# Two transformer layers in one kernel: the first attention stage, with its floor rows, small roots, key low parts and transfers put in another order

## The reference, cut to what matters

```python
x = x + L0_xattn(layernorm(x), ctx, ctx, ...)   # first stage: gated (mLSTM) attention
x = x + L0_ffn(layernorm(x), ...)               # silu(x wg) * (x wu), then wd
x = x + L1_xattn(layernorm(x), ctx, mask, ...)  # relu projections, softmax, weighted values
x = x + L1_ffn(layernorm(x), ...)               # ternary weights, two hidden layers

# inside L0_xattn, for each of 16 sequences and 8 heads:
ig, fg = (concat(q, k, v) @ w.T + b)                      # the gates
cs = cumsum(log_sigmoid(fg)); log_D = cs[s] - cs[t] + ig[t], causal
D = exp(log_D - max);  C = (q k^T / sqrt(32)) * D
h = C / (maximum(|sum C|, exp(-max)) + 1e-6) @ v          # exp(-max) is the "floor"
out = layernorm(h) * ln_scale
```

## Time and profile before

| | us |
|---|---|
| median of 3 runs (lowest, highest) | 562.78 (562.52, 564.67) |
| the profiled execution | 560.74 |
| its span, first to last instruction | 559.0 |
| TensorE busy | 538.2 |
| VectorE, ScalarE, GpSimd busy | 319.1, 243.4, 72.5 |

### The profile page before, as it was taken

One profiled execution on the slowest core, in us unless ns is written; L12 is line 12 of the kernel. 1 busy time (PEld: TensorE's weight loads), 2 busy tenths in 40 slices (PEclk: granted clock), 3 DMA queues, 4 the chain that ended last, 5 costly groups with the idle time before them and its releaser, 6 DMA issues.

```text
span 559.0 us, 8453 instructions
## 1 busy us (share of the span) xinstructions
PE 538.2 (96%) x2773; PEld 451.8 (81%) x2773; DVE 319.1 (57%) x776; ACT 243.4 (44%) x456; POOL 72.5 (13%) x116
## 2 busy tenths in 40 slices
PE   7899898999999999999999999999999999999996
PEld 5677777888998888778888788889788889788886
DVE  6678788868777689652443543434542543633333
ACT  6446657758798633551122441122541122631111
POOL 5232443204210441000000000000000000000000
PEclk9999999999999999999999999999999999999999
DMA  6693636356958776000000000000000000000001
GB/s 174 195 262 113 163 85 173 94 215 203 403 166 278 259 241 204 0 1 1 0 2 9 28 2 1 0 1 21 18 0 1 0 1 33 6 1 0 1 0 40
DMA packets 29860, 47.44 MB, mean 85 GB/s; under 512 B 3392, under 2 KB 21184, under 8 KB 29440
## 3 DMA queue, kind: packets, MB, share of 16 engines
q1 hardware_dynamic: 24848, 30.14, 17.1%
q0 software_dynamic: 4848, 16.78, 9.4%
q10 hardware_dynamic: 128, 0.05, 0.0%
HBM read 40.27 MB, written 2.10 MB: 76 GB/s over the span
## 4 chain that ended last, share of the span: by engine, by line
PE 59%; issue 8%; POOL 2%; DVE 1%; POOLq 0%; DVEq 0%
PE ps L953 58%; POOL rstd L457 1%; POOL h L575 1%; PE ps L609 0%; PE ps L917 0%; DVE qr L1595 0%; DVE x L1583 0%; DVE xn L1345 0%; DVE alT L1622 0%; DVE xT L1352 0%; POOL w L564 0%; POOLq L575 0%; POOL w L566 0%; PE ps L908 0%; DVE ot L1675 0%
## 5 line engine op out<-in xcount | busy, mean ns | idle before, releaser
L1308 ACT ACTIVATE h<-ps,scol 128x512 f32<-128x512 f32 x64 | 44.2, 690 | 175.3 <-PE ps L953 175.2
L953 PE MATMUL ps<-hBt,h 128*128 128x512 f32 x512 | 117.5, 390 | 0.0
L953 PE MATMUL ps<-hA,h 128*128 128x512 f32 x512 | 117.3, 390 | 0.0
L953 PEld LDWEIGHTS ps<-hA,h 128*128 128x128 f32 x512 | 95.9, 188 | 20.4 <-DVE hA L1649 0.6
L953 PEld LDWEIGHTS ps<-hBt,h 128*128 128x128 f32 x512 | 95.8, 188 | 20.3 <-DVE hBt L1649 0.6
L953 PE MATMUL ps<-xT,w 128*128 128x512 f32 x256 | 61.7, 396 | 1.0 <-DVE xT L1352 1.0
L953 PEld LDWEIGHTS ps<-xT,w 128*128 128x128 f32 x256 | 46.1, 188 | 14.9 <-issue 6.0
L1667 DVE CAST hBt<-h 128x512 fp32r<-128x512 f32 x32 | 13.7, 427 | 73.7 <-ACT h L1308 73.7
L1667 DVE CAST hA<-h 128x512 fp32r<-128x512 f32 x32 | 13.7, 427 | 70.0 <-ACT h L1308 70.0
L457 POOL TENSOR_TENSOR rstd<-ve,mhalf 128x4 f32<-128x4 f32 x16 | 16.4, 1028 | 263.1 <-DVE ve L1340 263.1
L1291 ACT ACTIVATE silD<-ps,scol 128x512 f32<-128x512 f32 x32 | 22.1, 689 | 45.1 <-PE ps L953 45.1
(11 more groups left out here) (180 smaller groups left out, 881.7 us busy)
## 6 DMA issues: line engine op xcount, KB each, us to landing
looked<-w_all_in SPq DMA_DIRECT2D x16, 704.0 KB, 5.9
h<-w_all_in POOLq DMA_DIRECT2D x16, 512.0 KB, 6.9
V<-ctx_in SPq DMA_DIRECT2D x8, 512.0 KB, 4.8
Qb<-xT SPq DMA_DIRECT2D x64, 64.0 KB, 2.0
w<-w_all_in POOLq DMA_DIRECT2D x3, 1024.0 KB, 7.0
x<-x_in SPq DMA_DIRECT2D x4, 512.0 KB, 4.7
kstA<-ctxT_in SPq DMA_DIRECT2D x4, 512.0 KB, 4.8
kstC<-ctxT_in SPq DMA_DIRECT2D x4, 512.0 KB, 6.9
```

Source lines behind the costliest of these rows:

```text
L953: last = mm(o, a, b, start=(k == 0 and p == 0), stop=(k == n_k - 1 and p == 1))
L1308: fn(h32[:, m % 2, :], ps[:, 2 + m % 4, :], ACT.Gelu, scale=scol[:, L + 1, m:m + 1])\
```

## The change

Six things move, and nothing is computed otherwise.

1. TensorE: `turn_e` of the next group stands behind the last scores of `q` = 3 instead of ahead of its exponent tiles. VectorE: `floor_copy` stands right ahead of the first `weigh` of `q` = 3 instead of behind `finish` in `q` = 2.
2. GpSimd: the layer norm's `nmean`, root and `shift`, and `h_root(Q*g, 0)`, stand ahead of the wait for the gates and of `pieces` instead of behind.
3. `k_lo` is two instructions of 512 columns, each with its semaphore, and the gates' keys wait for each half by itself.
4. SyncE: `x` of the last two groups is loaded ahead of the second keys instead of behind the first queries.
5. SyncE, in the loop: the queries of `q` = 2 stand ahead of the keys' load instead of behind.
6. SyncE, in the loop: the values' load stands behind the queries of `q` = 3 instead of ahead.

```diff
             sp.dma_start(diag[:, :], diag_in).then_inc(s["consts"], 16)
+            for g in range(2, G):
+                sp.dma_start(x[:, Q * g:Q * g + Q, :], x_in[Q * g:Q * g + Q].rearrange("b s d -> s b d"))\
+                    .then_inc(s["x_rest"], 16)
             sp.wait_ge(s["klo_done"], 1)
...
+                    queries_in(g, u, 2)
                     with sp.If(i < 1):
 
                         sp.wait_ge(s["klo_done"], 2 + u)
...
-                    queries_in(g, u, 2)
-                    def early():
+                    if u == 0:
                         gates_in(gn)
+                    else:
+                        with sp.If(i < 1):
+                            gates_in(gn)
+                    queries_in(g, u, 3)
+                    def following():
                         sp.wait_ge(s["pv_done"], Q * g + 2)
                         values(gn, 1 - u)
+                        lead_in(gn, 1 - u)
...
+            def k_lo_apart(n, u):
+
+                pool.wait_ge(s["khi_done"], n + 1)
+                for c, name in ((0, "klo_first"), (1, "klo_done")):
+                    nc.gpsimd.tensor_tensor(kT[:, u, 1, c, :], kstA[:, c, :], kT[:, u, 0, c, :], ALU.subtract)\
+                        .then_inc(s[name], 1)
...
                     if c == KD:
+                        pe.wait_ge(s["klo_first"], g + 1)
+                    if c == KD + 1:
                         pe.wait_ge(s["klo_done"], g + 1)
```

## The result

| | before | changed |
|---|---|---|
| median, 21 runs each (us) | 562.75 | 565.39 |
| lowest, highest | 559.08, 565.73 | 562.63, 568.07 |
| span of the profiled execution | 559.0 | 564.9 |
| granted TensorE clock, mean | 0.999 | 0.991 |

The ratio is 1.0054, 95% interval 1.0036 to 1.0072: slower by 3.0 us (2.0 to 4.0). The forecast was 561.5, no measurable change, with a range of 559.0 to 564.2: the measured time lies above it. One of the twelve executions of experiment 1 was slow (671.02 us, at a granted clock of 0.754) and is left out of its ratio.

A forecast was written before the change was run, and what follows sets the result against it. TensorE was busy 538.2 of 559.0 us, so only its idle time could be gained. Start -1.3, floor 0, halves -1.3, roots and transfers +1.3 made -1.3: 561.5 us from 562.78, range 559.0 to 564.2.

The forecast's parts named there:

- the roots first (edit 2) and the transfers' order (5, 6), +1.3: Starts of groups two to four: later weights slow the query transfers, 0.9, -0.2 and 0.6; the reordered transfers cost nothing; +1.3 us.
- the 0.4 of slack: Group starts: 0.2 us between queries landing and TensorE's scores, gained at two starts if the load has flowed.
- The rival that came true: Group starts: the load beside `lead_in` costs each 2.8 us, in rows and queries; +5.8, 568.6 us; chance 0.10.
- my sign of "slower": Profile after, group starts: query transfers landing in 4.8 us at all starts would mean the change is slower.
- all three starts would pay in full: Starts of groups two to four: if transfer engines take turns between queues, each pays the load's full cost, giving 568.6 us.
- The start (edit 4), -1.3: First group's start: with the `x` load moved, gate rows land at 23.84 instead of 25.37; gain taken as 1.3 us.
- my 24.0: First group's start: the profile after would show the first exponents at about 24.0 us.
- The floor rows (edit 1), 0: Ends of groups: TensorE stops waiting for floor rows but waits for queries instead; 0 by itself, ScalarE 0.8 us earlier.
- The halves (edit 3), -1.3: Third group's gates: keys' low parts in halves, with ScalarE 0.8 us earlier, remove TensorE's wait once; -1.3 us.
- the floor's argument: Group starts: TensorE arrives about 1.5 us earlier but then waits for the queries in place of the floor; gain 0.
- The transfers' order (5, 6), 0: SyncE's loop: costs nothing, as `V` and keys are wanted later; queries of `q` = 3 leave about 1.5 us earlier.
- my sum was -3.0: Whole kernel: with the weights' load harmless, +1.3 becomes -0.4, total -3.0, so 559.8 us; as a rival, chance 0.22.

The follow-up runs named there:

- experiment 1: The changed kernel with only the second edit taken back, so the second stage's weights go ahead of the roots again: 558.34 us, ratio 0.9933 to the kernel before.
- experiments 3: The changed kernel with only the first edit taken back, so the floor rows' turn stands ahead of the last exponents: 564.96 us, ratio 1.0058 to the kernel before.
- experiment 5: The changed kernel with the second stage's weights sent only when the next group's gate rows have landed: 569.05 us, ratio 1.0131 to the kernel before.
- experiment 2: The kernel before with the second edit alone, roots ahead of the second stage's weights: 566.84 us, ratio 1.0121 to the kernel before.

## Why the prediction was wrong

**The step that failed** is "the roots first (edit 2) and the transfers' order (5, 6), +1.3", in both halves. For edit 2 the place was right: the weights are sent at 37.84, as `h_root` of sequence 0 lets them, beside `lead_in`. Two sizes in it were wrong.
- *How long the load flows.* I took 4.2 us for 1.5 MB and 2.8 for 1 MB, from the 373 GB/s of a full microsecond, so most of it was to be gone when the queries leave. From the first issue to the last landing it is 9.0, 6.3 and 8.3 us at the three starts (37.84 to 46.9, 65.13 to 71.4, 88.19 to 96.5). The trace of the kernel before had it: issued from 35.60 on, the last of the four at 37.44 and 6.3 us in flight (lines below), so 8.1.
- *What is in flight with it.* I priced the queries alone, 0 to 2.8 a start. The gate rows leave with the load and land with its end, 7.4, 4.0 and 5.9 us after the issue of the last (39.76, 67.99, 90.66), where 2.8 was enough in quiet. That rows can be late beside a load stood in the trace as well: 4.0 at the start.

Of the kernel before, GpSimd's last weights in the first group, and the same transfer's size and time to landing:

```profile
37.44 0.53 POOL L494 DMA_DIRECT2D rawd<-l0d_in  x1
```

```profile
rawd<-l0d_in POOLq DMA_DIRECT2D x1, 384.0 KB, 6.3
```

Measured, edit 2 costs 6.8 us (5 to 8.5 by the intervals), where I had 1.7 (1.3 and the 0.4 of slack).

**The clock had no term.** I treated an idle microsecond as one. Two idle times of 3.8 and 2.2 us put the clock to 1.2 GHz for some 7 and 3 us. They cost 3.8 us in the profiled execution; filling the first got back 2.2 of them, and 2.6 in the runs.

**The rival that came true** is the slower one, "the load beside `lead_in` costs every group start 2.8, in rows and queries alike", with 0.10. Its place was right. Its size was not (+5.8 against +3.0): I had it at three starts, and the middle one, with 1 MB, waits 0.43; the queries are not waited for at all, although they take the 4.8 (4.4 in the fourth group) that was my sign of "slower", because the rows are later still; and half of the loss is the clock's, which the rival did not have either. The rule of the Trainium skill that I set against the forecast ("DMA: Bandwidth & Descriptors", section "Queues, rings and completion order": transfer engines take turns between queues a packet at a time) pointed the right way, though no run here shows packets taking turns; "all three starts would pay in full", which I drew from it, did not come true at the middle one.

**The start (edit 4), -1.3:** right. The first exponents moved by 1.0 in the profile (24.41; 23.99 and 23.89 in experiments 3 and 5, against my 24.0). The runs give 2.8 alone (1.8 to 3.8), of which 1.1 is left among executions at full clock, and 1.9 in company, with some 2 to either side.

**The floor rows (edit 1), 0:** right. The waits vanish from the list and nothing is gained, since the next group's rows and queries do not come sooner.

**The halves (edit 3), -1.3:** not seen. The wait for low parts goes, and the next start waits for gate rows instead. It was the floor's argument, which I had made one paragraph before and not applied here.

**The transfers' order (5, 6), 0:** wrong. I asked when `V` and the keys are wanted, and not who stands behind them. The queries of `q` = 3 need 2.0 ahead of `V` and 4.3 behind it, and edit 1 makes TensorE want them 1.5 earlier. Worth 2.5 us alone (1.1 to 3.9) and 3.1 in company, with some 2 to either side. In company the waits of 3.10 and 1.42 show how; alone it is not shown.

With edit 2 taken out, my sum was -3.0, and 3.8 was measured (2.4 to 5.2). That they agree is luck: 1.3 for the halves was not there, and some 3 for the order were missing.

**Left open:** why the gate rows land only with the end of the load, when queries sent behind them land before it; what decides whether the clock falls behind a wait; and where the kernel before loses its clock in the executions that have no trace.

## What to carry to other kernels

A big load's place in a queue is a decision about all small transfers that are in flight with it. Before you put a wait in front of a load, write down what will be issued while it flows. Take that time from the trace, from its first issue to its last landing (8 to 9 us for 1.5 MB here), and not from its size and the highest GB/s. Price each kind of transfer by its own row, not by that of a neighbour. The other half of this change is the cheap remedy, small transfers on the path ahead of big ones that are not: moved so, two reorderings brought 0.4 and 0.5% (intervals 0.2 to 0.7 and 0.3 to 0.7). And a wait of TensorE may cost as much again in clock behind it: look at the granted clock in the microseconds after each new wait, and if it can't be avoided, fill it. Last, compare the mean clock of all executions before you lean on one profile: here the profiled execution of the kernel before was one of its faster ones, and most others had a lower clock.

## What was not expected of the hardware

Small transfers beside a load take two to three times as long: 64 KB of queries to 32 partitions 4.8 to 5.8 us instead of 2.0, the last 16 KB of gate rows, to 4 partitions, 7.4 and 5.9 instead of 2.8. The smaller transfer was the slower one in quiet (2.8 against 2.0) and in the changed kernel's second and fourth group (7.4 against 4.8, 5.9 against 4.4). The Trainium skill has a rule that may bear on it ("DMA: Bandwidth & Descriptors", section "Rules for kernel authors": an outermost dimension of fewer than 16 confines a transfer to at most that many transfer engines); no run here shows how many engines the rows used. And the length of an idle time does not alone tell whether the clock falls: it fell in the company of waits of 1.87, 2.24 and 3.84 us, and it stayed at 1.00 behind the 2.38 of experiment 2 and, in experiment 5, behind 3.56 us at 46.84.
